# Deeper rings and another order of the tiles in two sparse expert layers of an eight-layer kernel

## What is computed

```python
x = x + _L2_xattn_ref(_layernorm(x, axis=-1), ctx_1024, ...)
x = x + _L2_ffn_ref(_layernorm(x, axis=-1), ...)

def _L2_xattn_ref(x, context, Wg, bg, W1, b1, W2, b2):    # E = 8, K = 2, FFN = 512
    logits = jnp.einsum('bsd,de->bse', context, Wg) + bg
    scores_topk, idx_topk = jax.lax.top_k(logits, K)
    weights = jax.nn.softmax(scores_topk, axis=-1)
    combine = jnp.sum(jax.nn.one_hot(idx_topk, E, dtype=weights.dtype) * weights[..., None], axis=-2)
    h = jax.nn.relu(jnp.einsum('bsd,edf->bsef', x, W1) + b1)
    y = jnp.einsum('bsef,efd->bsed', h, W2) + b2
    return jnp.einsum('bsed,bse->bsd', y, combine)

def _L2_ffn_ref(x, w_router, w_gate, w_up, w_down):       # 8 experts, TOP_K = 2, 352 hidden
    ...
    gate = jax.nn.silu(jnp.einsum('th,eih->eti', xf, w_gate))
    up = jnp.einsum('th,eih->eti', xf, w_up)
    down = jnp.einsum('eti,ehi->eth', gate * up, w_down)
    out = jnp.einsum('eth,te->th', down, combine)
```

## Time and profile before

| what | us |
|---|---|
| median of the runs | 961.72 |
| the three runs | 966.69, 961.72, 960.16 |
| profiled execution, from its first to its last instruction | 1010.8 |
| PE busy in it | 783.2 |
| DVE busy | 608.2 |
| ACT busy | 486.4 |
| POOL busy | 372.9 |

### The profile page before, as it was taken

The page is one execution under the profiler, slowest core; times in us unless marked ns, Lnnn a source line. Parts: engine busy times, 40 slices in busy tenths (PEclk is TensorE's granted clock), DMA queues, the critical chain, the costliest instruction groups (busy, mean ns, idle before and its releaser), DMA issues.

```text
span 1010.8 us, 24129 instructions
## 1 busy us (share of the span) xinstructions
PE 783.2 (77%) x8041; PEld 646.4 (64%) x8041; DVE 608.2 (60%) x1568; ACT 486.4 (48%) x984; POOL 372.9 (37%) x492
## 2 busy tenths in 40 slices
PE   6998899999999789996477775667677559969005
PEld 3766787888888679985476664667676526644005
DVE  3886747777777667767353224632222368867895
ACT  3886434555444344432154435334444357745753
POOL 5663421111111331111566653155556535550810
PEclk9999699999999979999699989579989769978557
DMA  6300000000000000033332213101111300000001
GB/s 187 96 0 1 1 1 3 2 3 0 0 0 3 1 11 19 21 102 103 95 100 88 64 41 105 42 19 43 40 37 45 85 23 3 0 1 1 0 0 42
DMA packets 49218, 36.06 MB, mean 36 GB/s; under 512 B 7665, under 2 KB 44978, under 8 KB 49138
## 3 DMA queue, kind: packets, MB, share of 16 engines
q1 hardware_dynamic: 43420, 24.45, 8.5%
q0 software_dynamic: 4992, 10.23, 3.6%
q10 hardware_dynamic: 726, 0.33, 0.1%
HBM read 26.73 MB, written 8.26 MB: 35 GB/s over the span
## 4 chain that ended last, share of the span: by engine, by line
PE 67%; DVE 9%; another core or an unknown queue 6%; issue 5%; ACT 5%; DMA 3%; DVEq 2%; POOL 2%; ACTq 1%; SPq 1%; POOLq 0%
PE psum L2118 9%; PE psum L1464 7%; PE psum L2143 4%; PE psum L1034 3%; PE psum L976 3%; PE psum L954 3%; PE psum L939 3%; PE psum L2442 2%; PE psum L1431 2%; PE psum L1432 2%; PE psum L1433 2%; PE psum L323 2%; PE psum L1016 2%; PE psum L663 2%
## 5 line engine op out<-in xcount | busy, mean ns | idle before, releaser
L2118 PE MATMUL psum<-E_XT,E_weights 128*128 128x128 f32 x780 | 114.3, 298 | 52.4 <-ACT E_XT L2198 27.7
L2118 PEld LDWEIGHTS psum<-E_XT,E_weights 128*128 128x128 f32 x780 | 103.0, 209 | 61.2 <-ACT E_XT L2198 30.8
L2266 POOL DMA_INDIRECT y_scratch<-E_y,route_place_of x78 | 78.8, 1010 | 83.2 <-DVE E_y L2321 37.8
L2258 POOL DMA_INDIRECT E_rows<-rows_scratch,route_token_of x78 | 76.4, 979 | 32.1 <-issue 25.5
L1723 DVE SCALAR_TENSOR_TENSOR X<-psum,E_gates,X 128x128 f32<-128x128 f32 x256 | 71.7, 344 | 26.5 <-PE psum L1464 26.4
L1464 PEld LDWEIGHTS psum<-E_w,E_h 128*128 128x128 f32 x512 | 69.4, 198 | 11.5 <-issue 3.5
L2221 ACT ACTIVATE E_h<-psum,cols 128x128 f32<-128x128 f32 x156 | 44.5, 368 | 66.4 <-issue 31.3
L1548 ACT ACTIVATE E_h<-psum,cols 128x512 f32<-128x512 f32 x64 | 43.8, 687 | 67.8 <-PE psum L1433 67.7
L1464 PE MATMUL psum<-E_w,E_h 128*128 128x128 f32 x512 | 70.4, 282 | 4.8 <-DVE X L1723 3.8
L2311 DVE TENSOR_TENSOR E_h<-E_sg,psum 128x384 f32<-128x384 f32 x39 | 21.6, 554 | 77.5 <-remote 26.8
L203 POOL TENSOR_TENSOR rstd<-vareps,nhalf 128x4 f32<-128x4 f32 x24 | 24.6, 1029 | 75.0 <-DVE vareps L197 74.9
(11 more groups left out here) (346 smaller groups left out, 2160.2 us busy)
## 6 DMA issues: line engine op xcount, KB each, us to landing
routed_back<-y_scratch SPq DMA_DIRECT2D x16, 256.0 KB, 4.9
E_first<-in_L_xattn_W SPq DMA_DIRECT2D x1, 2048.0 KB, 8.6
L1w<-in_L_xattn_W SPq DMA_DIRECT2D x8, 256.0 KB, 4.7
rows_scratch<-xn SPq DMA_DIRECT2D x8, 256.0 KB, 2.3
E_w<-in_L_ffn_routed_w SPq DMA_DIRECT2D x28, 64.0 KB, 1.9
E_raw<-in_L_ffn_w_down SPq DMA_DIRECT2D x8, 176.0 KB
E_rows<-rows_scratch,route_token_of POOLq DMA_INDIRECT x78
y_scratch<-E_y,route_place_of POOLq DMA_INDIRECT x78
```

Source lines behind the costliest of these rows:

```text
L2118: mm = pe.matmul(out[:, c * P:(c + 1) * P], WE[:, p, (k0 + c) * P:(k0 + c + 1) * P], XT[:, p, :], start=True, stop=True)
L2258: pool.indirect_dma_start(out=xg[:, i % 4, :], out_offset=None, in_=rows[:, :], in_offset=bass.IndirectOffsetOnAxis(ap=disp.token_of[:, i: ...
L2266: pool.indirect_dma_start(out=yrows[:, :], in_=y[:, i % 3, :], in_offset=None, out_offset=bass.IndirectOffsetOnAxis(ap=disp.place_of[:, i: ...
```

## The change

The rings become deeper: eight buffers for gathered rows (`ROWS = 8`), four each for `XT`, `WE`, `h` and `y` (`RING = 4`). `h` now lies in the normalised rows `m.xn`, which the first gather of the layer has already waited for to be stored, and E2's `WE` lies in `m.XNT`, the transposed activations. PE turns tiles two ahead of the first products (`AHEAD = 2`) and makes the second products three tiles behind them (`BEHIND = 3`). POOL issues eight gathers before the first scatter. The turns of raw weights are no longer one in each of 24 iterations, but one at each third half of an iteration, over iterations 1 to 36. What every engine computes, and the number of DMAs, matmuls and copies, stay.

```diff
+RING, ROWS = 4, 8
+AHEAD, BEHIND = 2, 3
...
-        xg, XT = sb("rows", [P, 4, D]), sb("XT", [P, 2, TILE])
-        h, y = sb("h", [P, 2, C, TILE]), sb("y", [P, 3, D])
-        WE = sb("weights", [P, 2, W1.shape[2]])
+        xg, XT, y = sb("rows", [P, ROWS, D]), sb("XT", [P, RING, TILE]), sb("y", [P, RING, D])
         if gated:
-            sg = sb("sg", [P, 2, C, TILE])
+            WE, sg = sb("weights", [P, RING, W1.shape[2]]), sb("sg", [P, 2, C, TILE])
+        else:
+            WE = m.XNT[:, :].rearrange("p (r f) -> p r f", r=RING)
...
+    h = m.xn[:, 0:RING * C, :].rearrange("p (r c) s -> p r c s", c=C)
...
-    def turned_at(n):
-
-        return n - 2 if turns and 0 <= n - 2 < 3 * turns.E else None
+    def turned_at(i, half):
+
+        q, rest = divmod(2 * i + half - 2, 3)
+        return q if turns and rest == 0 and 0 <= q < 3 * turns.E else None
...
-        turn(0)
-        for i in range(NTILE):
-            first(i)
-            if i + 1 < NTILE:
-                turn(i + 1)
-            if i >= 1:
-                second(i - 1)
-            if turned_at(i) is not None:
-                turns.turn(pe, turned_at(i))
-        second(NTILE - 1)
+        for i in range(AHEAD):
+            turn(i)
+        for i in range(NTILE + BEHIND):
+            if i < NTILE:
+                first(i)
+            if i + AHEAD < NTILE:
+                turn(i + AHEAD)
+            if turned_at(i, 0) is not None:
+                turns.turn(pe, turned_at(i, 0))
+            if i >= BEHIND:
+                second(i - BEHIND)
+            if turned_at(i, 1) is not None:
+                turns.turn(pe, turned_at(i, 1))
...
             act.wait_ge(*xT_ps(i + 1))
-            if i >= 2:
-                act.wait_ge(*a_ps(2 * i - 2))
-            act.activation(XT[:, i % 2, :], T[i % 2][:, 0:P], ACT.Copy).then_inc(xT_ready.sem, 1)
+            if i >= RING:
+                act.wait_ge(*a_ps(2 * (i - RING + 1)))
+            act.activation(XT[:, i % RING, :], T[i % 2][:, 0:P], ACT.Copy).then_inc(xT_ready.sem, 1)
...
             for i in range(NTILE):
+                if turned_at(i - 1, 1) is not None:
+                    turns.keep(act, turned_at(i - 1, 1))
                 hidden(i)
-                if turned_at(i) is not None:
-                    turns.keep(act, turned_at(i))
+                if turned_at(i, 0) is not None:
+                    turns.keep(act, turned_at(i, 0))
...
         def fetch(i):
-            if i >= 4:
-                pool.wait_ge(*xT_ps(i - 3))
+            if i >= ROWS:
+                pool.wait_ge(*xT_ps(i - ROWS + 1))
...
-        for i in range(3):
-            fetch(i)
-        for i in range(NTILE + 2):
-            if i + 3 < NTILE:
-                fetch(i + 3)
-            if i >= 2:
-                send(i - 2)
+        for i in range(ROWS - 1):
+            fetch(i)
+        for i in range(NTILE):
+            if i + ROWS - 1 < NTILE:
+                fetch(i + ROWS - 1)
+            send(i)
...
-        for i in range(NTILE):
-            if gated:
+        for i in range(NTILE + BEHIND):
+            if gated and i < NTILE:
                 hidden(i)
-            elif i + 1 < NTILE:
-                weights(i + 1)
-                rows_turned(i + 1)
-            if i >= 1:
-                output(i - 1)
+            if not gated and i + AHEAD < NTILE:
+                weights(i + AHEAD)
+                rows_turned(i + AHEAD)
+            if i >= BEHIND:
+                output(i - BEHIND)
             if "prepare" in spec and i >= 4:
                 spec["prepare"](dve, i - 4)
-        output(NTILE - 1)
```

More of the change, by code:

```diff
@@ L2049, in dispatched_experts @@
     T, Y, J1 = m.banks[0:2], m.banks[6:8], m.banks[1]
+    hid, gate_banks, up_banks = m.banks[2:5], m.banks[2:4], m.banks[4:6]
     rows, yrows = m.rows_dram, m.y_dram
@@ L2056, in dispatched_experts @@
     rows_stored = signal("routed_rows_stored", 16 * NG)
-    x_here = [signal(f"routed_rows_here{k}", 16 * uses(4, k)) for k in range(4)]
+    x_here = [signal(f"routed_rows_here{k}", 16 * uses(ROWS, k)) for k in range(ROWS)]
     xT_ps, xT_ready = signal("routed_rows_turned", NTILE), signal("routed_rows_split", NTILE)
@@ L2061, in dispatched_experts @@
     y_ps, y_out = signal("routed_y_in_psum", NTILE), signal("routed_y", NTILE)
-    y_sent = [signal(f"routed_y_sent{k}", 16 * uses(3, k)) for k in range(3)]
+    y_sent = [signal(f"routed_y_sent{k}", 16 * uses(RING, k)) for k in range(RING)]
     y_here = [signal(f"routed_y_here{g}", 32) for g in range(NG)]
@@ L2083, in sync @@
                 turns.load(sp, e)
-        for k in range(3):
-            sp.wait_ge(*y_sent[k](16 * uses(3, k)))
+        for k in range(RING):
+            sp.wait_ge(*y_sent[k](16 * uses(RING, k)))
         for g in range(NG):
@@ L2122, in first @@
         def first(i):
-            p = i % 2
+            p = i % RING
             pe.wait_ge(*xT_ready(i + 1))
@@ L2128, in first @@
                     pe.wait_ge(*h_ready(i - 1))
-                products(m.banks[2 + p], p, 0)
-                products(m.banks[4 + p], p, C)
+                products(gate_banks[i % 2], p, 0)
+                products(up_banks[i % 2], p, C)
             else:
@@ L2133, in first @@
                     pe.wait_ge(*h_ready(i - 2))
-                products(m.banks[2 + i % 3], p, 0)
+                products(hid[i % 3], p, 0)
         def second(i):
-            p = i % 2
+            p = i % RING
             e = pe.value_load(disp.expert[0:1, i:i + 1], min_val=0, max_val=E - 1)
@@ L2226, in scalar @@
             act.wait_ge(*spec["weights_here"])
-            weights(0)
-            rows_turned(0)
+            for i in range(AHEAD):
+                weights(i)
+            for i in range(AHEAD):
+                rows_turned(i)
             for i in range(NTILE):
-                if i + 1 < NTILE:
-                    weights(i + 1)
+                if i + AHEAD < NTILE:
+                    weights(i + AHEAD)
                 silu(i)
-                if i + 1 < NTILE:
-                    rows_turned(i + 1)
+                if i + AHEAD < NTILE:
+                    rows_turned(i + AHEAD)
             disp.gate_exps(act)
@@ L2255, in fetch @@
         def fetch(i):
-            if i >= 4:
-                pool.wait_ge(*xT_ps(i - 3))
-            pool.indirect_dma_start(out=xg[:, i % 4, :], out_offset=None, in_=rows[:, :],
+            if i >= ROWS:
+                pool.wait_ge(*xT_ps(i - ROWS + 1))
+            pool.indirect_dma_start(out=xg[:, i % ROWS, :], out_offset=None, in_=rows[:, :],
                                     in_offset=bass.IndirectOffsetOnAxis(ap=disp.token_of[:, i:i + 1], axis=0)
-                                    ).then_inc(x_here[i % 4].sem, 16)
+                                    ).then_inc(x_here[i % ROWS].sem, 16)
         def send(i):
@@ L2265, in send @@
                 pool.wait_ge(*disp.place_ready(1))
-            pool.indirect_dma_start(out=yrows[:, :], in_=y[:, i % 3, :], in_offset=None,
+            pool.indirect_dma_start(out=yrows[:, :], in_=y[:, i % RING, :], in_offset=None,
                                     out_offset=bass.IndirectOffsetOnAxis(ap=disp.place_of[:, i:i + 1], axis=0)
-                                    ).then_inc(y_sent[i % 3].sem, 16)
-        for i in range(3):
+                                    ).then_inc(y_sent[i % RING].sem, 16)
+        for i in range(ROWS - 1):
             fetch(i)
-        for i in range(NTILE + 2):
-            if i + 3 < NTILE:
-                fetch(i + 3)
-            if i >= 2:
-                send(i - 2)
+        for i in range(NTILE):
+            if i + ROWS - 1 < NTILE:
+                fetch(i + ROWS - 1)
+            send(i)
     def vector(dve):
@@ L2328, in vector @@
             dve.wait_ge(*spec["weights_here"])
-            weights(0)
-            rows_turned(0)
-        for i in range(NTILE):
-            if gated:
-                hidden(i)
-            elif i + 1 < NTILE:
-                weights(i + 1)
-                rows_turned(i + 1)
-            if i >= 1:
-                output(i - 1)
+            for i in range(AHEAD):
+                weights(i)
+            for i in range(AHEAD):
+                rows_turned(i)
+        for i in range(NTILE + BEHIND):
+            if gated and i < NTILE:
+                hidden(i)
+            if not gated and i + AHEAD < NTILE:
+                weights(i + AHEAD)
+                rows_turned(i + AHEAD)
+            if i >= BEHIND:
+                output(i - BEHIND)
             if "prepare" in spec and i >= 4:
                 spec["prepare"](dve, i - 4)
-        output(NTILE - 1)
         disp.gates(dve)
```

49 lines of the change are left out of this document (24 added, 25 removed).

## The result

The changed kernel takes 972.55 us (median of four runs, 970.85 to 974.89), the kernel before 961.15 in the runs beside it. The ratio is 1.0107 with a 95% interval from 1.0077 to 1.0137. Measured once more, beside other runs of the kernel before, the changed kernel took 970.26 against 963.2, a ratio of 1.0066 (1.0034 to 1.0098). It is slower, by 7 to 11 us or 0.7 to 1.1%. The forecast was 965, 4 us slower, with a range of 930 to 979.

What follows compares the result with a forecast made beforehand. POOL's DMA issues with their 0.30 us gaps were taken to bound both sparse layers. Start +1.5 and +1.9, tail +1.5 twice and steady state -2.4 gave +4.0 on 961.7, forecast 965 us, range 930 to 979.

Steps and rivals of the forecast that it cites:

- What bounds the kernel: Both sparse layers: POOL's issues with their gaps set the least time; timed runs already at most 10.5 us above it.
- the late completions: PE's results seen 2.5 to 2.9 us late by VectorE and ScalarE in the profiled sparse layers; few in timed runs.
- The 49 us between span and median: Profiled span 1010.8 against timed median 961.72, at least 49.1 us less; nearly the 55.6 of the chain's unknown part.
- Steady state: Between fill and tail of both layers: longer path hidden, no cost; deeper rings win 0 to 4.8 us, middle -2.4.
- POOL's floors: Sparse layers if each output wait were only the 0.30 gap: 102.7 and 100.6 us, 203.3 together.
- Start: First scatter of each layer waits longer for output 0: +1.5 us in E2, +1.9 in E3.
- Tail: After the last gather, eight scatters left instead of six; POOL waits 2.2 instead of 0.7 us, +1.5 each layer.
- Sum: Start, tail and steady-state terms together: +4.0 us on timed runs, 965.7, given as 965, chance 0.53.
- Late completions in the timed runs: Rival: PE's late results also cost timed runs, and its larger lead bridges them; 935 us, chance 0.26.
- Slower by scatter n behind the turn of tile n + 5: Rival: late completions eat the smaller cover in steady state, so POOL waits for outputs; 986 us, chance 0.14.
- the cover: POOL's issue time from gather n+5 to scatter n beyond the path's need: 1.2 to 1.5 us, before 4.1.
- Gaps at no cost: Rival: POOL's 0.30 us gaps cost nothing in timed runs, PE's busy time limits; 948 us, chance 0.07.

Runs made afterwards that it cites:

- E2: Not a run: tag of the first sparse layer, from first gather to last scatter; 131.10 us in the first profile, 108.2 in experiment 1.
- experiment 1: The kernel before, unchanged, profiled anew; 962.52 us.
- experiment 8: The changed kernel with ten gathers ahead instead of eight and second products one tile behind instead of three; 952.93 us, ratio to before 0.9883.
- E3: Not a run: tag of the second sparse layer, from first gather to last scatter; 131.80 us in the first profile, 103.9 in experiment 1.
- experiment 9: The changed kernel with seven gathers ahead instead of eight, turns two ahead and second products three behind as they are; 1030.77 us, ratio to before 1.0693.
- experiment 10: The kernel of experiment 8 with one more POOL instruction, a small memset, ahead of each scatter; 954.68 us, ratio to before 0.9918.

## Why the prediction was right, and where it was not

*What bounds the kernel.* Right, and shown: the timed execution that was profiled had none of the late completions, and the others took as long; POOL's rate of one DMA in 1.28 us sets both layers (experiments 1 and 8). The 49 us between span and median were the key to it. I put the layers at 213.8 in a timed run; experiment 1 has 212.1. One sign that I named was wrong: the late completions should still have stood in the profile of after, with a span 10 to 30 us shorter. They were gone, and the span was 41 us shorter.

*Steady state: no cost, -2.4 as the middle of 0 to -4.8.* No cost was right in the main: with eight gathers no wait, or at most 1.1 us a layer. The -2.4 was wrong. Of what the layers had above POOL's floors I gave 5.7 us to the fill and left the rest to be won by deeper rings. But most of the rest was the old kernel's own tail, 2.1 and 1.6 us beyond the gaps, of which I had seen about 0.7 a layer and which I had not taken off here. There was nothing to win: between its first scatter and its last gather the kernel before has no wait longer than 0.32.

*Start: +1.5 and +1.9.* Right in kind, and too high. In E2 the first scatter waits 3.1 and 4.3 in the two profiles, not 5.3, against 3.9 and 0.2 at a gather before: -1.0 and +0.2. The first products ran at the upper clock sooner than I took: the four ahead of second products 0 take 1.92, 1.40, 1.06 and 1.06 us in the first profile and 1.92, 1.92, 1.70 and 1.06 in the second, so that the two that are new cost little. In E3 4.5 and 3.4, not 5.1, against 2.2 and 0.7: +1.5 and +0.4. Both layers together: +0.5 and +0.6, where I had +3.4.

*Tail: +1.5 each.* Right: 3.45 against 2.1 in E2 and 3.7 against 1.6 in E3, so +1.4 and +2.1, and by the mechanism named. Both levels are higher than I worked out (2.2 and 0.7), their difference is not.

*Sum: +4.0.* The layers grew by 5.0 in the first profile and 5.2 in the second (110.98 + 106.36 less 212.1). That the sum came so near is partly luck: the start was 2.8 to 2.9 us too high, and the 2.4 that I took off for the steady state did not exist; the two errors nearly cancel. The measured +7 to +11 has 2 to 6 us more than the layers. Of these one execution shows 4.5 in the stretch behind E3, together with the fall of the clock in the next attention; the prediction had no term for what stands outside the layers. What the rest of the difference is, and why the two measurements differ, stays open. I gave a slowdown of over 1% a chance of 0.15; the first measurement is there (1.07%), the second is not (0.66%).

*The rivals.* Late completions in the timed runs: fallen (experiment 1). Slower by scatter n behind the turn of tile n + 5: not at eight gathers, but one gather less makes it true and costs 60 us (experiment 9). The path is 4.9 us at its shortest, as I worked out, but I took no account of tiles with a longer one: in the two profiles of the changed kernel scatter n could have started 5.3 to 5.9 us after gather n + 5 (medians of the layers), so the cover was nearer 0.5 to 1.1 than 1.2 to 1.5. Gaps at no cost: half fallen. A layer can't be shorter than its DMAs with their gaps, but other work of POOL fits into these (experiment 10). The rule of the Trainium skill ("Perfetto Trace Analysis", section "Identifying the Most-Contended Engine"), that GpSimd's occupancy is a fair measure of how close it is to its limit, does not hold here for these DMAs: in experiment 8 POOL can issue no more of them, and is busy 78.3 of 101.7 us, 77%.

## What to carry to other kernels

A lag between stages is paid for twice, when the pipeline fills and when it empties, and can be of use only where something in steady state waits. Before making one deeper, look whether the bound engine waits there at all, and count how many of its instructions cover the fill and the drain: here eight gathers cover a lag of one tile nearly, ten cover it wholly, and for a lag of three not even ten suffice. When the bound engine does wait in steady state, remember that the wait for one tile also covers part of the next tile's path: what a path is too long by is not paid for every tile. And where a profile's span is longer than the timed runs, its waits may be that execution's alone: profile the kernel again before designing against them.

## What the runs showed of the hardware that I had not expected

POOL's gap of 0.30 us between two of its DMA instructions takes in a memset of 0.139 us: 78 of them, 10.8 us of work, made the two layers 0.6 us longer in the profiles (201.8 against 201.2), and in the lines shown the DMA behind a memset does not start later.

One execution of the kernel before had completions of PE that ACT and DVE saw late, by 2.5 to 2.9 us in the earlier trace rows, again and again through both sparse layers, which took 50.8 us longer than in experiment 1. Twelve other profiled executions, of the same kernel and of changed ones with the same DMAs, had none like it.
